# Latent self attentions of a Perceiver: heads in pairs of 64-row operands, both sequences in one run

## The reference, cut to what matters

```
def L0_attn(x):                      # x: (2, 256, 256), head size 16
    q, k, v = heads(x @ Wq.T + bq), heads(x @ Wk.T + bk), heads(x @ Wv.T + bv)
    scores = einsum('bqhd,bkhd->bhqk', q, k) / 4
    pos_emb = dist_emb[511 + pos_q[:, None] - pos_k[None, :]]        # (256, 256, 16)
    scores = scores + einsum('bqhd,qkd->bhqk', q, pos_emb)
    scores = scores + einsum('bkhd,qkd->bhqk', k, pos_emb)
    return einsum('bhqk,bkhd->bqhd', softmax(scores), v)             # x = x + this

def L2_attn(x):                      # rotary q and k, causal, then Wo and an MLP
    scores = where(causal, -inf, einsum('bhqd,bhkd->bhqk', q, k) / 4)
    return einsum('bhqk,bhkd->bhqd', softmax(scores), v) @ Wo + bo
```

## Time and profile before

| | |
|---|---|
| median of the runs | 4079.12 us |
| the profiled execution | 4080.47 us, its span 4078.7 us |
| busy in the span | PE 84%, PEld 52%, DVE 57%, ACT 37%, POOL 20% |
| layer 0, from its first load to that of the next stage | 240.39 to 473.91 us |
| layer 2, likewise | 3001.59 to 3106.38 us |

### The profile page before, as it was taken

How to read it: one execution, slowest core, us unless ns; L and a number is a source line. 1 busy time by engine, 2 the same in 40 slices (tenths; PEclk the granted TensorE clock), 3 DMA queues, 4 the chain that set the end, 5 groups by cost and what they waited for, 6 DMA issues and landing times. The chain is left out here.

```text
span 4078.7 us, 55851 instructions
## 1 busy us (share of the span) xinstructions
PE 3406.9 (84%) x21132; PEld 2130.0 (52%) x21188; DVE 2315.1 (57%) x3897; ACT 1529.1 (37%) x2241; POOL 810.1 (20%) x572
## 2 busy tenths in 40 slices
PE   7878895999999699999759587899857579995759
PEld 5546684656656466566525375444446434442225
DVE  1144413655655656656368413899654279984963
ACT  2223311334334243343246321467633137773311
POOL 0000000254255152453218202000000110000420
PEclk9888897999999799999879788999977789997879
DMA  2245463000000100000187513765200285540001
GB/s 94 85 142 181 166 238 140 16 6 6 6 1 1 55 6 9 4 4 1 30 272 260 218 68 105 164 122 106 50 21 26 103 205 114 120 81 21 0 22 59
DMA packets 223953, 339.07 MB, mean 83 GB/s; under 512 B 104272, under 2 KB 177680, under 8 KB 218064
## 3 DMA queue, kind: packets, MB, share of 16 engines
q1 hardware_dynamic: 223312, 334.56, 28.1%
q0 software_dynamic: 384, 1.05, 0.1%
HBM read 257.95 MB, written 77.63 MB: 82 GB/s over the span
## 5 line engine op out<-in xcount | busy, mean ns | idle before, releaser
L1428 DVE TENSOR_REDUCE L1x_pk<-L1x_psm 128x1 f32<-128x512 f32 (+1 forms) x576 | 374.8, 661 | 177.1 <-PE L1x_psm L1259 170.0
L1229 POOL TENSOR_TENSOR L1x_acc<-L1x_acc,L1x_pr 128x512 f32<-128x512 f32 x256 | 416.4, 1627 | 137.3 <-ACT L1x_pr L1404 118.9
L1404 ACT ACTIVATE L1x_pr<-L1x_pss 128x1024 f32<-128x1024 f32 x272 | 278.6, 1024 | 285.4 <-PE L1x_pss L1316 277.8
L1450 DVE TENSOR_TENSOR L1x_acc<-L1x_acc,L1x_pr 128x512 f32<-128x512 f32 x256 | 261.1, 1020 | 202.0 <-ACT L1x_pr L1404 197.6
L955 DVE TENSOR_REDUCE L2x_pk<-L2x_psm 128x1 f32<-128x512 f32 x512 | 328.1, 685 | 38.1 <-PE L2x_psm L792 34.3
L955 DVE TENSOR_REDUCE L3x_pk<-L3x_psm 128x1 f32<-128x512 f32 x512 | 328.1, 685 | 32.5 <-PE L3x_psm L792 28.7
L932 ACT ACTIVATE L2x_pr<-L2x_pss 128x1024 f32<-128x1024 f32 x256 | 248.2, 1021 | 105.6 <-PE L2x_pss L833 105.3
L932 ACT ACTIVATE L3x_pr<-L3x_pss 128x1024 f32<-128x1024 f32 x256 | 248.1, 1021 | 100.6 <-PE L3x_pss L833 100.3
L1316 PE MATMUL L1x_pss<-L1x_Q,L1x_K 64*128 64x256 f32 x2176 | 279.3, 376 | 0.0
L1282 PE MATMUL L1x_pss<-L1x_w,L1x_cT 128*128 128x256 f32 x1088 | 278.4, 380 | 0.8
L1277 PE MATMUL L1x_pss<-L1x_cT,L1x_w 128*128 128x512 f32 (+1 forms) x576 | 277.4, 572 | 0.8
(11 more groups left out here) (653 smaller groups left out, 5991.2 us busy)
## 6 DMA issues: line engine op xcount, KB each, us to landing
f0e_wt<-in_f_pieces SPq DMA_DIRECT2D x10, 3072.0 KB, 11.4
offset_rows<-s_rows SPq DMA_DIRECT2D x32, 768.0 KB, 3.4
L2x_KS<-L2x_key_parts SPq DMA_DIRECT2D x24, 1024.0 KB, 13.1
L3x_KS<-L3x_key_parts SPq DMA_DIRECT2D x24, 1024.0 KB, 13.1
s_add<-offset_rows SPq DMA_DIRECT2D x32, 512.0 KB, 3.8
n_cT<-in_ctxT SPq DMA_DIRECT2D x32, 512.0 KB, 5.3
f1e_wt<-in_f_pieces SPq DMA_DIRECT2D x8, 2048.0 KB, 15.0
L2x_key_parts<-n_kst SPq DMA_DIRECT2D x32, 384.0 KB, 3.1
```

The lines of the kernel that those rows point to most:

```text
L1229: i = nc.gpsimd.tensor_tensor(acc[:, n, 1, :, :], acc[:, n, 1, :, :], pr[:, A % RING, :, 1, :], ALU.add)
L1404: nc.scalar.activation(pr[:, A % RING, :, :, :].rearrange("p h e q -> p (h e q)"), pss[:, x:x + 2, :].rearrange("p h n -> p (h n)"), ACT.E ...
L1428: nc.vector.reduce_max(pk[:, m, hq, j:j + 1], psm[:, i % 2, 0:NQ[j][1]], AX).then_inc(peak_read, 1)
L1450: i = nc.vector.tensor_tensor(acc[:, n, 0, :, :], acc[:, n, 0, :, :], pr[:, A % RING, :, 0, :], ALU.add)
```

## The change

`self_attention` is written anew; `layer0_self` and `layer2_self` call it as before.

- The loop over the sequences is gone: both sequences' 32 heads run in one stage, in 16 pairs. `LAG` is counted in pairs and is 2 for layer 0.
- A pair has one head in partitions 0 to 63 and one in 64 to 127 of the same chunk. Products and scores take 64-row slices of the masked operands, one for each head, into different PSUM banks.
- The masks are made by GpSimd, in a ring of 8 heads in layer 0 (`MR`), and for all 32 heads in layer 2.
- `psr` has one bank per head of the pair. ScalarE copies all four products of the first head, VectorE those of the second. `sc` and `add` have four buffers.
- `products` are spread between scores, averages and turns, and each waits for the copies of the one before.
- SyncE stores both heads of a pair, then loads both heads of the pair before.
- In layer 0 `normalize` adds straight into `X`; `O` and `add_to` are gone there. Layer 2 uses `kT` and `V` themselves, not copies.

```
-    with nc.Fori(0, B) as b, Tensors(nc) as t:
+    N = B * NH
+    PAIRS = N // 2
+    MR = 8 if relative else N
+    LAG = 2 if relative else 0
...
+                def store(n):
+                    sp.wait_ge((rel_act, rel_dve)[n % 2], 4 * (n // 2 + 1))
+                    sp.dma_start(scratch[n % NH].rearrange("x p w -> p x w"), rows[:, n % 4, :, :]).then_inc(outs[n % 4], 16)
+                def shifted(n):
+                    sp.wait_ge(outs[n % 4], 16 * (n // 4 + 1))
+                    if n >= 4:
+                        sp.wait_ge(summed, n - 3)
+                        sp.wait_ge(scored, (n - 4) // 2 + 1)
...
+                    sp.dma_start(add[:, n % 4, :, :], skew).then_inc(adds[n % 4], 16)
+                for p in range(PAIRS + 1):
+                    if p < PAIRS:
+                        store(2 * p)
+                        store(2 * p + 1)
+                    if p >= 1:
+                        shifted(2 * p - 2)
+                        shifted(2 * p - 1)
...
+                for n in range(N):                      # GpSimd
+                    b, h, c, r = where(n)
+                    if n >= MR:
+                        pool.wait_ge(scored, (n - MR) // 2 + 1)
+                    nc.gpsimd.tensor_scalar(qz[:, n % MR, :], qT[:, c, b * S:(b + 1) * S], mask[:, h % HPC:h % HPC + 1], None, ALU.mult).then_inc(masked, 1)
...
+                def products(p, x):
+                    side, i = divmod(x, 2)
+                    if x == 0:
+                        pe.wait_ge(masked, 4 * (p + 1))
+                    if 4 * p + x >= 1:
+                        pe.wait_ge(rel_act, 4 * p + x)
+                        pe.wait_ge(rel_dve, 4 * p + x)
+                    for r in range(2):
+                        part = slice(64 * r, 64 * r + 64)
+                        nc.tensor.matmul(psr[:, r, 0:RW], (qz, kz)[side][part, (2 * p + r) % MR, i * P:(i + 1) * P],
+                                         emb[part, side, P * (1 - i):P * (1 - i) + RW], start=True, stop=True).then_inc(rel, 1)
+                def scores(p):
...
+                        for r in range(2):
+                            pe.wait_ge(adds[(2 * p + r) % 4], 16 * ((2 * p + r) // 4 + 1))
...
+                    if p >= 1:
+                        pe.wait_ge(summed, 2 * p)
...
+                for p in range(PAIRS + LAG + 2):        # TensorE; s, t, a = p - LAG, p - LAG - 1, p - LAG - 2
+                    products(p, 0); scores(s); products(p, 1); average(2 * a); average(2 * a + 1)
+                    products(p, 2); turn(2 * t); products(p, 3); turn(2 * t + 1)
...
+                for p in range(PAIRS + LAG + 2):        # VectorE
+                    copy_row(p, 0); total(2 * s); copy_row(p, 1); total(2 * s + 1)
+                    copy_row(p, 2); normalize(2 * a); copy_row(p, 3); normalize(2 * a + 1)
...
+                for p in range(PAIRS + LAG + 2):        # ScalarE
+                    copy_row(p, 0); copy_turned(2 * a + 1); exponentials(2 * t); copy_row(p, 1)
+                    exponentials(2 * t + 1); copy_row(p, 2); copy_turned(2 * t); copy_row(p, 3)
...
-        add_to(nc, k.X, O, "s0a")
```

More of the change, by code:

```diff
@@ L2590, in self_attention @@
             pso = u.ps(pre + "_pso", [P, 2, 512])
[L2591 to L2594, removed]
+            psr = u.ps(pre + "_psr", [P, 2, 512])
             @block.sync
             def _(sp):
+                sp.dma_start(mask[:, :], d["mask16"]).then_inc(load, 16)
                 if not relative:
-                    sp.dma_start(mask[:, :], d["mask16"]).then_inc(load, 16)
                     sp.dma_start(add[:, 0, 0:QT, :], d["causal"]).then_inc(load, 16)
[L2601 to L2620, removed]
@@ L2658, in average @@
[L2658 to L2666, removed]
@@ L2668, in products @@
[L2668 to L2704, removed]
@@ new lines, in _ @@
+                for p in range(PAIRS + LAG + 2):
+                    s, t, a = p - LAG, p - LAG - 1, p - LAG - 2
+                    if relative and p < PAIRS:
+                        products(p, 0)
+                    if 0 <= s < PAIRS:
+                        scores(s)
+                    if relative and p < PAIRS:
+                        products(p, 1)
+                    if a >= 0:
+                        average(2 * a)
+                        average(2 * a + 1)
+                    if relative and p < PAIRS:
+                        products(p, 2)
+                    if 0 <= t < PAIRS:
+                        turn(2 * t)
+                    if relative and p < PAIRS:
+                        products(p, 3)
+                    if 0 <= t < PAIRS:
+                        turn(2 * t + 1)
@@ new lines, in normalize @@
+                def normalize(n):
+                    b, h, c, r = where(n)
+                    dve.wait_ge(av, n + 1)
+                    link(nc.vector.reciprocal(rec[:, n, :], sums[:, n, :]))
+                    for qt in range(QT):
+                        o = O[:, b * QT + qt, h * hd:(h + 1) * hd]
+                        part = pso[:, n % 2, qt * hd:(qt + 1) * hd]
+                        if relative:
+                            nc.vector.scalar_tensor_tensor(o, part, rec[:, n, qt:qt + 1], o, ALU.mult, ALU.add).then_inc(scaled, 1)
+                        else:
+                            nc.vector.tensor_scalar(o, part, rec[:, n, qt:qt + 1], None, ALU.mult).then_inc(scaled, 1)
@@ new lines, in _ @@
+                dve.wait_ge(load, 32)
+                for p in range(PAIRS + LAG + 2):
+                    s, a = p - LAG, p - LAG - 2
+                    for r in range(2):
+                        if relative and p < PAIRS:
+                            copy_row(p, r)
+                        if 0 <= s < PAIRS:
+                            total(2 * s + r)
+                    for r in range(2):
+                        if relative and p < PAIRS:
+                            copy_row(p, 2 + r)
+                        if a >= 0:
+                            normalize(2 * a + r)
@@ new lines, in copy_row, with exponentials @@
+                def copy_row(p, x):
+                    n = 2 * p
+                    if x == 0:
+                        rows_free(act, n)
+                    act.wait_ge(rel, 8 * p + 2 * x + 1)
+                    nc.scalar.copy(rows[:, n % 4, x, :], psr[:, 0, 0:RW]).then_inc(rel_act, 1)
+                def exponentials(n):
+                    act.wait_ge(peak, n + 1)
+                    if n >= 2:
+                        act.wait_ge(turned, n - 1)
+                    for qt in range(QT):
+                        nc.scalar.activation(pr[:, n % 2, qt, :], sc[:, n % 4, qt, :], ACT.Exp, bias=nm[:, n, qt:qt + 1], scale=SC,
+                                             accum_out=sums[:, n, qt:qt + 1]).then_inc(expd, 1)
```

219 lines of the change are left out of this document (115 added, 104 removed).

## The result

The changed kernel takes 4180.26 us (median of 4 runs, 4166.07 to 4181.95) against 4078.56 for the kernel before beside it: a ratio of 1.024, 95% interval 1.0221 to 1.0259. The forecast was 4160, in a range of 4112 to 4210. The profiled execution took 4181.95 us with a span of 4179.5, 100.8 more than before.

What follows compares the result with a forecast made beforehand. Layer 0 was taken as bound by PE, layer 2 by VectorE. 4080.47 + 104.4 (layer 0) - 22.9 (layer 2) = 4162.0 us profiled, which stands 1.35 above the median, so 4160, range 4112 to 4210.

Steps and rivals of the forecast that it cites:

- The chain of layer 0: Layer 0: scores wait for loads queued behind the previous pair's stores, a closed chain of 20.3 us a pair, against 12.0.
- (a): Layer 0 round, from the end of the scores to the last row copy: 6.0 us.
- (b): Layer 0 round, from the last row copy until the `add` loads have landed behind the stores: 9.3 us.
- (c): Layer 0 round, scores and key terms on PE with three shape changes of 0.1 each: 2.9 us.
- (d): Layer 0 round, extra time because PE's clock falls in the idle wait: 2.1 us.
- Layer 0 in all: Whole stage of layer 0, start, rounds and tail, ending at 578.3 against 473.9: +104.4 us.
- Layer 2: Whole stage of layer 2, bound by VectorE, 14 pairs at 4.40 us, ending at 3083.5 against 3106.38: -22.9 us.
- The clock stays up: Rival, layer 0: PE's clock does not fall in the wait, 31 us less, 4129; chance 0.10.
- low all round: Rival, layer 0: PE's clock stays low through the whole round, 50 us more, 4210; chance 0.13.
- Halves do not overlap: Rival, layer 0: 64-row operands do not run at once, 2.2 us more a round, 4195; chance 0.03.
- Loads overtake: Rival, layer 0 queue: loads pass the stores, 2.9 us less a round, 44 less in all, 4116; chance 0.07.
- The other side: Rival, layer 0: `add` loads are there when PE asks, a round is 9.8 us, 4003, faster; chance 0.06.

Runs made afterwards that it cites:

- experiment 4: Changed kernel with ten extra 128x448 matmuls between a pair's first product and the scores in layer 0: 4144.21 us, ratio 1.0159.
- experiment 1: Changed kernel with SyncE issuing the loads of the pair before ahead of this pair's stores in layer 0: 4039.03 us, ratio 0.9893.
- experiment 6: Changed kernel with layer 2's scores taken on all 128 rows instead of 64: 4173.88 us, ratio 1.0222.
- experiment 3: Changed kernel with each head's rows stored twice, first to a scratch area nobody reads, and loads waiting for both: 4224.65 us, ratio 1.0341.
- experiments 7 and 11: Layer 0 as in the kernel before, layer 2 as changed: 4076.34 us; the same with layer 2's first four pairs' scores on full rows: 4068.05 us.
- experiments 5 and 8: Changed kernel with five 128x512 products ahead of layer 2's first scores: 4180.75 us; the same with layer 0's loads ahead of stores: 4035.62 us.

## Why the prediction was right, and where its sizes were off

**The chain of layer 0** was as the prediction had it, link by link. (a) 408.17 to 414.1 is 5.95, forecast 6.0. (b) 414.1 to 422.90 is 8.8, forecast 9.3: the stores ran at 400 GB/s and only the turn to loads fell to 230, so the 332 of the earlier trace rows was a little low. (c) at full clock is 3.44 by experiment 4, forecast 2.9: a group of eight key terms takes 1.09 from start to start (336.30 to 337.39 in experiment 1) instead of 0.87, so by this estimate a change between halves and full rows cost 0.2, not the 0.1 read from the earlier trace rows. The Trainium skill, "TensorEngine Tiling (Array Packing)", section "Key Properties", says that changing the tiling mode drains TensorE; the 0.2 agrees with that, though no run here separates it from another cost of the change. (d) is 2.3, forecast 2.1: the clock was back 5 us after the work began (422.90 to 428) and not after 3.6. The round is 20.5 (14 rounds from 278.60 to 566.44, 287.8 us, mean 20.56), forecast 20.3. It is nearer than its terms by luck: (b) was 0.5 too high and (c) 0.5 too low. One sign was wrong: the four issues took 3.5 us (414.02 to 417.56), not some 1.5, and the loads landed 6.5 us after their issue in the median, where the forecast had 8 to 9 for the second.

**Layer 0 in all** came to +115.9 for +104.4. The 11.5 us more are 2.7 at the start (a mask takes 0.92, not 0.75, and cold product blocks 2.4, not 2.0 to 2.3: 250.66 to 269.94 for eight), 3.6 in the rounds, and 5.2 in the tail, mostly where the clock fell once more: the last averages took 3.60 us, against 1.86 at a clock of 1.00.

**Layer 2** is the term that was mis-sized the most: "then 14 pairs at 4.40", with the clock up after the first of them. It gained 10.1, not 22.9. Of the 12.8 us missing, the start has 1.6 (1.1 of it ahead of GpSimd's first mask at 3113.11) and the first two pairs 1.6; three pairs at 7.32 instead of 4.40 have 8.8; a tail at the low clock has 5.1 (in 1.4 of them no engine works any more: 2.5 us from the last normalization to the next stage, forecast 1.1); and 11 pairs at 4.00 give 4.4 back. The pair at 4.00 is two totals at 1.51 and two normalizations at 0.49, which the earlier trace rows had at 0.67 each. The earlier trace rows showed the clock up 4 us after the first matmul and I took it for granted; what they show was true of scores on full rows.

**The rivals.** "The clock stays up" and "low all round" both fell: it was 0.50 for the scores and 1.00 by the next product. "Halves do not overlap" fell: the eight score records of a pair take 1.2 us in experiment 1 (0.56 + 0.63), where full rows took 1.8 in experiment 6. "Loads overtake" fell with experiment 3. The other side, 4003, became true in kind once the loads were issued a pair earlier: experiment 1 has 10.18 a round, where the rival said 9.8.

**The rest of the program**, which the sum put at nothing, was 5.1 us shorter, and that is not only scatter. From the end of layer 0 to the start of layer 2 the program took 2514.5 to 2523.1 us in all eleven profiles with the new layer 0, and 2527.6 to 2529.9 in the three with the old one (the kernel before, experiments 7 and 11). The code between is the same in both, and why it runs faster behind the new layer 0 stays open. The forecast was 19.2 us short in the profiles: 11.5 in layer 0 and 12.8 in layer 2, less these 5.1.

## What to carry to other kernels

When work is batched, look at the issue list of the queue and count which transfers now stand behind the last product of the same round: two lines changed places turned a loss of 2.4% into a gain of 1.1%. An operand that halves TensorE's cycles is worth nothing where another engine or a transfer sets the pace. After a gap, read the granted clock of the stretch itself and not of a similar one with other shapes.

## What was not expected of the hardware

TensorE stayed at a granted clock of 0.50 (1.2 GHz) for 33 to 48 us, in the changed kernel with 10 of 10 us busy from the third pair on, in five of eight executions in which the scores were on 64-row halves, and scores on full rows in the first pairs were followed by a rise within 11 us in five of five. A rise bought with five added products was lost 5 us later (experiments 5 and 8). While GpSimd made masks, VectorE's smallest operation, the negated maximum of 128x2, lasted up to 0.60 us instead of 0.17. ScalarE's exponentials wait for it, but TensorE was busy in 10 of 10 us (3125 to 3135) and did not; GpSimd itself took 0.92 us for 128x256.
